# Steps of three batches moved in an attention and expert kernel, with another order of loads and turned copies at the end

## The reference

```python
def _L0_xattn_ref(query, key, value, adj, mask, ...):      # 16 heads of 16
    Q, K, V = heads(query, Wq, bq), heads(key, Wk, bk), heads(value, Wv, bv)
    scores = jnp.einsum('bhqd,bhkd->bhqk', Q, K) / jnp.sqrt(jnp.float32(D))
    scores = scores + adj[None, None, :, :]
    scores = jnp.where(mask == 0, jnp.float32(-jnp.inf), scores)
    weights = jax.nn.softmax(scores, axis=-1)
    out = jnp.einsum('bhqk,bhkd->bhqd', weights, V)
    out = out.transpose(0, 2, 1, 3).reshape(b, s, E)
    return jnp.einsum('bsf,ef->bsf', out, Wo.T) + bo

def _L0_ffn_ref(hidden_states, gate_w, w1, b1, w2, b2):    # 8 experts, 256 -> 1024 -> 256
    gate_probs = jax.nn.softmax(x @ gate_w.T, axis=-1)
    expert_idx = jnp.argmax(gate_probs, axis=-1)
    expert_w = jnp.take_along_axis(gate_probs, expert_idx[:, None], axis=1)[:, 0]
    for e in range(n_experts):
        ye = jax.nn.relu(x @ w1[e] + b1[e]) @ w2[e] + b2[e]
        sel = (expert_idx == e)[:, None]
        out = out + jnp.where(sel, ye * expert_w[:, None], 0.0)

x = x + jnp.tanh(g_xattn[0]) * _L0_xattn_ref(_layernorm(x), ctx, ctx, adj, mask, ...)
x = x + jnp.tanh(g_ffn[0]) * _L0_ffn_ref(_layernorm(x), gate_w, w1, b1, w2, b2)
```

## Time and profile before

| | |
|---|---|
| median of three runs | 571.88 us (569.12 to 575.5) |
| profiled execution | 572.78 us, a span of 570.8 us |
| mean granted clock of TensorE | 0.996 of full |
| TensorE matmul busy | 532.1 us, 93% of the span |
| TensorE weight load busy (beside matmul) | 405.8 us, 71% |
| VectorE, ScalarE, POOL busy | 298.7, 304.6, 304.2 us, 52 to 53% each |
| data moved | 77.22 MB, mean 135 GB/s |

### The profile page before, as it was taken

One profiled execution on the slowest core, in us unless ns is written; L12 is line 12 of the kernel. 1 busy time (PEld: TensorE's weight loads), 2 busy tenths in 40 slices (PEclk: granted clock), 3 DMA queues, 4 the chain that ended last, 5 costly groups with the idle time before them and its releaser, 6 DMA issues.

```text
span 570.8 us, 13582 instructions
## 1 busy us (share of the span) xinstructions
PE 532.1 (93%) x4126; PEld 405.8 (71%) x4127; DVE 298.7 (52%) x908; ACT 304.6 (53%) x675; POOL 304.2 (53%) x461
## 2 busy tenths in 40 slices
PE   7999999989999989999999998879997899999996
PEld 5576666657566657666666765548897899999995
DVE  2676677875577876576876878813510111111111
ACT  4466676666677566678665676443232233333331
POOL 6345476765466665467573646451425445544441
PEclk9999999999999999999999999989999999999999
DMA  8633526301216410105510078778137656555650
GB/s 280 206 107 101 170 87 201 103 20 48 101 39 201 131 41 1 76 18 167 177 49 1 28 247 213 161 258 313 57 37 279 195 166 163 189 196 192 198 186 6
DMA packets 51392, 77.22 MB, mean 135 GB/s; under 512 B 9945, under 2 KB 34601, under 8 KB 51209
## 3 DMA queue, kind: packets, MB, share of 16 engines
q1 hardware_dynamic: 46600, 67.72, 37.2%
q0 software_dynamic: 4096, 8.29, 5.2%
q10 hardware_dynamic: 640, 0.52, 0.3%
HBM read 52.76 MB, written 7.89 MB: 106 GB/s over the span
## 4 chain that ended last, share of the span: by engine, by line
PE 51%; DMA 18%; issue 10%; DVE 7%; POOL 5%; ACT 4%; SPq 4%; POOLq 1%; DVEq 0%; ACTq 0%
PE bank L941 13%; DMA out_y<-cT,sidx 10%; PE bank L953 9%; PE bank L931 7%; PE bank L834 4%; DVE prob L1551 3%; DMA slot_d<-pair,posi 3%; SPq L345 3%; PE bank L1116 2%; PE bank L869 2%; PE bank L915 2%; PE bank L1031 2%; PE bank L1106 2%; ACT pt L1209 2%; POOL rows L739 2%
## 5 line engine op out<-in xcount | busy, mean ns | idle before, releaser
L1551 DVE CUSTOM_DVE_ANT_0 prob<-bank,adjm 128x512 f32<-128x512 f32 x256 | 172.5, 687 | 82.1 <-issue 50.1
L672 POOL TENSOR_SCALAR prob<-prob,negmax 128x512 f32<-128x512 f32 x192 | 133.2, 698 | 130.6 <-DVE negmax L1551 125.7
L1209 ACT ACTIVATE pt<-bank 128x512 f32<-128x512 f32 x256 | 150.3, 594 | 87.6 <-PE bank L941 83.3
L941 PE MATMUL bank<-ident,prob 128*128 128x128 f32 x1024 | 154.8, 274 | 4.6 <-POOL prob L672 2.3
L941 PEld LDWEIGHTS bank<-ident,prob 128*128 128x128 f32 x1024 | 124.2, 141 | 43.5 <-issue 14.7
L1278 ACT ACTIVATE adjm<-bank,colsm 128x128 f32<-128x128 f32 x184 | 52.6, 368 | 107.5 <-PE bank L1106 86.0
L931 PE MATMUL bank<-w2s 128*128 128x512 bf16 x256 | 97.5, 381 | 7.6 <-DVE negmax L1551 4.9
L953 PE MATMUL bank<-pt,vals 128*32 128x256 f32 x1024 | 69.1, 389 | 0.7 <-DVE vals L1365 0.5
L1727 DVE TENSOR_TENSOR cT<-bank,maski 128x256 f32<-128x256 f32 x18 | 7.6, 424 | 117.3 <-PE bank L1116 103.3
L1106 PEld LDWEIGHTS bank<-xT,pt 128*128 128x128 f32 x576 | 67.1, 192 | 1.8 <-ACT xT L1272 1.0
L1106 PE MATMUL bank<-xT,pt 128*128 128x128 f32 x576 | 67.3, 275 | 0.7 <-ACT xT L1272 0.7
(11 more groups left out here) (192 smaller groups left out, 604.0 us busy)
## 6 DMA issues: line engine op xcount, KB each, us to landing
pt<-in_L_ffn_w SPq DMA_DIRECT2D x19, 1024.0 KB, 5.2
w2s<-parts SPq DMA_DIRECT2D x96, 128.0 KB
w2s<-in_L_ffn_w SPq DMA_DIRECT2D x8, 1024.0 KB, 9.9
maski<-in_mask_Bx1xSxS_ik SPq DMA_DIRECT2D x4, 1024.0 KB, 5.4
w2s<-parts SPq DMA_DIRECT2D x56, 64.0 KB, 2.1
xres<-in_x SPq DMA_DIRECT2D x18, 128.0 KB, 2.2
x_d<-rows SPq DMA_DIRECT2D x18, 128.0 KB, 1.7
xn_d<-rows SPq DMA_DIRECT2D x18, 128.0 KB, 2.5
```

What stands on the lines that cost most here:

```text
L672: po.tensor_scalar(prob[:, m], prob[:, m], -1.0, negmax[:, m:m + 1], ALU.mult, ALU.add).then_inc(s_shpool, 1)
L941: mm = pe.transpose(tr_bank[n % NTB][:, c * P:(c + 1) * P], prob[:, n % TILES % NB, c * P:(c + 1) * P], ident[:])
L1209: act.activation(pt[:, g % 2, :, j, q2 * P:(q2 + 1) * P], tr_bank[c % NTB][:].rearrange("p (c q) -> p c q", c=QT), ACT.Exp).then_inc(s_cac ...
L1551: ve.tensor_tensor_reduce(out=prob[:, m % NB], in0=sc_bank[m % NS][:], in1=adjm[:, qt], scale=-1.0, scalar=BIG, op0=ALU.add, op1=ALU.min, ...
```

## The change

In the first three batches, by the tables:

- the use "turn 1" goes from step 25 to 26, and "next k 0" from 26 to 27;
- "gate 0,1" goes from step 43 to 44, and "gate 3" from 66 to 68;
- the four slot scatters go from steps 53, 55, 57, 59 to 54, 59, 62, 67, and the wait for them from 72 to 73;
- the factor for the next but one batch's x goes from step 66 to 67, its normalization from 67, 69, 71, 73 to 69, 70, 72, 73.

In the last batch one slot scatter goes from step 45 to 46. At the end SP issues three w1 loads of the early groups ahead of the five slot reads (before: one ahead, two behind) and the w2 of experts 4 and 6 behind them (before: ahead of them). TensorE turns the rows of early group 1 ahead of the second half of the hidden layer of group 0, and ScalarE copies them in the same place. The first two w1 loads of the late groups go ahead of the first two late slot reads, and so ahead of the wait for the last scatters.

```diff
--- before.py
+++ after.py
@@ -94,14 +94,14 @@
     PRE = len(PRO)
     FIRST_NEXT = PRO.index("next x")
     NEXT = 8
-    TAIL_A = [(15, "heads", 0), (18, "heads", 1), (23, "turn", 0), (25, "turn", 1), (29, "out", 0),
-              (33, "out", 1), (38, "normed", 0), (41, "normed", 1), (43, "gate", (0, 1)), (51, "rank", 0)]
+    TAIL_A = [(15, "heads", 0), (18, "heads", 1), (23, "turn", 0), (26, "turn", 1), (29, "out", 0),
+              (33, "out", 1), (38, "normed", 0), (41, "normed", 1), (44, "gate", (0, 1)), (51, "rank", 0)]
     USES = sorted([(10, "values", 0), (11, "values", 1)] + TAIL_A
                   + [(12, "next x", 0), (14, "next x", 1), (17, "next ctx", 0), (19, "next ctx", 1),
-                     (21, "next q", 0), (26, "next k", 0), (30, "next q", 1), (35, "next k", 1)]
+                     (21, "next q", 0), (27, "next k", 0), (30, "next q", 1), (35, "next k", 1)]
                   + [(45, "heads", 2), (46, "heads", 3), (50, "turn", 2), (52, "turn", 3), (53, "out", 2),
                      (56, "out", 3), (61, "normed", 2), (63, "gate", (2,)), (64, "normed", 3),
-                     (66, "gate", (3,))], key=lambda use: use[0])
+                     (68, "gate", (3,))], key=lambda use: use[0])
     LAST_USES = sorted([(10, "values", 0), (11, "values", 1), (13, "heads", 0), (14, "heads", 1), (16, "turn", 0),
                         (18, "turn", 1), (20, "out", 0), (22, "out", 1), (27, "normed", 0), (29, "normed", 1),
                         (31, "gate", (0, 1)), (39, "rank", 0), (45, "heads", 2), (46, "heads", 3), (48, "turn", 2),
@@ -115,11 +115,11 @@
     OUT_RSTD = ({32: 0, 36: 1, 56: 2, 59: 3}, {23: 0, 25: 1, 55: 2, 57: 3})
     ROW_STEPS = ({36: 0, 39: 1, 59: 2, 63: 3}, {25: 0, 27: 1, 57: 2, 59: 3})
     SHIFT_STEP, EXP_STEP, PICK_STEPS = (45, 33), (46, 34), ((47, 48, 49), (35, 36, 37))
-    STATS_STEPS, RSTD_STEP, NORM_STEPS = (61, 62, 64, 65), 66, (67, 69, 71, 73)
+    STATS_STEPS, RSTD_STEP, NORM_STEPS = (61, 62, 64, 65), 67, (69, 70, 72, 73)
     CAST_STEPS = {n + VE_QK_AT + 1: (i, w, a) for i, (n, w, a) in enumerate(USES)
                   if w in ("next q", "next k")}
     SPLIT_STEPS = {n + 1: use for n, use in CAST_STEPS.items()}
-    SLOT_STEPS, SCATTERED_STEP = ((53, 55, 57, 59), (41, 43, 45, 47)), (72, 60)
+    SLOT_STEPS, SCATTERED_STEP = ((54, 59, 62, 67), (41, 43, 46, 47)), (73, 60)
     TABLE_STEPS = (41, 42, 43, 44, 45, 48, 49, 50, 51, 52, 57, 58)
     INDEX_STEP, NORMED_STEPS = TILES - 5, (TILES - 5, TILES - 2)
     ABS_STEPS = {29: 0, 34: 1, 40: 2, 45: 3}
@@ -479,18 +479,17 @@
                 sp.dma_start(ew1[u], w1_v[ds(e, 1)].rearrange("x p k f -> p (x k) f")).then_inc(e_w1[u], 16)
 
             sp.wait_ge(s_stack, last * STACKED)
-            sp.wait_ge(s_score, last * TILES + 6 * TILES // 8)
-            for e in range(X // 2, X, 2):
-                load_w2(e)
             sp.wait_ge(e_eid, 1)
-            early_w1(0)
+            sp.wait_ge(s_xT, B * 4)
+            for s in range(3):
+                early_w1(s)
             sp.wait_ge(r_scat, B * (16 * QT))
             for s in range(EARLY):
                 at = sp.value_load(base_i[0:1, s:s + 1], min_val=0, max_val=X * TOK)
                 sp.dma_start(slots[:, s], slot_d[ds(at, P), :]).then_inc(e_slots, 16)
-            sp.wait_ge(s_xT, B * 4)
-            for s in range(1, 3):
-                early_w1(s)
+            sp.wait_ge(s_score, last * TILES + 6 * TILES // 8)
+            for e in range(X // 2, X, 2):
+                load_w2(e)
             tail_pair(last, last * QT, 2, last * QT + 2)
             sp.wait_ge(s_score, B * TILES)
             for e in range(X // 2 + 1, X, 2):
@@ -520,11 +519,11 @@
                 sp.dma_start(w1s[:, v], w1_v[ds(e, 1)].rearrange("x p k f -> p (x k) f")).then_inc(f_w1[v], 16)
 
             sp.wait_ge(r_eid, 1)
+            for v in range(2):
+                load_w1(v, v)
             sp.wait_ge(r_scat, (B + 1) * (16 * QT))
             for v in range(2):
                 load_slots(v, v)
-            for v in range(2):
-                load_w1(v, v)
             with sp.Fori(0, LATE // 2 - 1) as i:
                 for v in range(2):
                     load_slots(i * 2 + (v + 2), v, i * 2 + v + 1)
@@ -1060,8 +1059,8 @@
             pe.wait_ge(s_osb, B * GROUPS + 2)
             last_tail("heads", 0)
             last_tail("heads", 1)
+            early_turn(1)
             early_hidden(0, 1)
-            early_turn(1)
             last_tail("turn", 0)
             last_tail("turn", 1)
             early_hidden(1, 0)
@@ -1294,8 +1293,8 @@
             act.wait_ge(e_eid, 1)
             e = expert_of(0)
             hidden(0, 0, e, 0)
+            turned_rows(1, 1)
             hidden(0, 0, e, 1)
-            turned_rows(1, 1)
             last_tail("turn", 0)
             last_tail("turn", 1)
             e = expert_of(1)
```

## The result

The change makes the kernel slower: 584.95 us (median of 4 runs, 583.37 to 588.54) against 571.66 us, a ratio of 1.024 with a 95% interval of 1.019 to 1.029. Run again with more rounds it gave 585.97 us and 1.025 (1.021 to 1.030). The forecast was 575 us with a range of 565 to 582: the time lies above it. The profiled execution has a span of 581.5 us, 10.7 more than before, and a clock of 0.991. Lines of the changed kernel are one lower than before from about 480 on.

The account below looks back on a forecast made before the run. TensorE was taken as the bound in the batches, chains of scatter, slot reads and gather at the end. +6.5 us in three batches and -3.7 at the end gave +2.8 on 572.78, or 575 us against the median, range 565 to 582.

Parts of the forecast that it names:

- The two moved uses: Three batches: new waits at "next q 1" and "next k 1", 1.75 then 3.83 us late in all; +11.5 us together.
- Gates, slot scatters, normalization: Three batches: waits at gates, behind slot scatters and for rstd go or shrink: -2.7, -1.5 and -0.8 us.
- The clock at the new waits: Slower rival: one clock fall of 1.8 us per batch at the new waits, none saved at the end; 581 us, chance 0.08.
- Late w1 loads ahead of the late slot reads ... I take 0: Late groups: loads leave the gather's time and enter the scatter's; taken as 0, between +1.9 and -2.8 us.
- The early end: Early groups: index -0.8, gather -1.0, clock -0.9, turned copy of slot 1 -1.0; together -3.7 us.
- The gather, taken 1.0 us shorter: After the early slot reads: 7.55 us before, now beside two other loads; -1.0 us, between 0 and -3.85.
- The estimate of when the loads would be in: Early end: 3.1 MB of w1 loads ahead of the slot reads all in at about 370.9 us.
- The gain of 0.8 us for the index: Early slot reads behind three w1 loads: index 0.8 us earlier, between -1.78 and +2.7.
- the fit that the prediction set beside this: Early w1 loads: 2.0 us plus bytes over 436 GB/s, in after 9.2 us at 368.5; sum 1.0 us lower.
- The sum: Whole kernel: +6.5 us in three batches, -3.7 at the end, +2.8 in all; 575 us against the median.
- The two slower rivals: Clock falls at the new waits, 581 us, chance 0.08; slot reads come late behind loads, 582 us, chance 0.10.
- reads behind loads (the late ones): Slower rival: slot reads late behind loads, +2.7 for -0.8, no gather or clock gain, +1.9 at late reads; chance 0.10.

Follow-up runs that it names:

- a_moves_back: The changed kernel with "turn 1" put back to step 25 and "next k 0" to 26, late order kept: 572.31 us, 1.000 to before.
- b_moves_only: The kernel before with only "turn 1" at step 26 and "next k 0" at 27: 582.36 us, 1.017 to before.
- change_again: The whole change run once more with more rounds, against the kernel before: 585.97 us, 1.025.
- a_both_back: The changed kernel with the two uses back at 25 and 26 and the late w1 loads back behind the late slot reads: 566.9 us, 0.992 to before.
- b_moves_steps: The kernel before with the two uses, gates, slot scatters and normalization moved, the whole end as before: 584.23 us, 1.017 to before.
- b_late_act: The kernel before with the first two late w1 loads issued by ScalarE on its own queue, ahead of early group 4's hidden layer: 577.1 us, 1.011 to before.

## Why the prediction was wrong, point by point

- **The two moved uses: right in mechanism, place and size.** 3.83 us per batch was the working; 3.67 to 3.71 was measured. Each link (tile, `rows`, `rest`; shift, factor, split) stood in the trace, and the two kernels that reorder VectorE and POOL took one wait away and cut the other.
- **Gates, slot scatters, normalization: near.** -5.0 was forecast; the batches of a_moves_back are 1.67, 1.52 and 1.37 us shorter than before, -4.6. The kernel with these steps alone gained 3.4 us.
- **The clock at the new waits: the wrong side of the choice.** I gave this rival 0.08 because the clock had held beside the 2.77 us ahead of the late loop. That was the exception: in eight of the other nine profiles with the old order of the late reads it fell at this place. After the wait of 2.0 us in the batches it fell in 8 of the 12 batches of the four profiles that have it together with the moved steps, and in none of the three of b_moves_only, which I can't explain. The price, 1.8 us, was right: 1.6 and 1.8 for the same batch with and without a fall. One execution in which the clock held says little about the next.
- **"Late w1 loads ahead of the late slot reads ... I take 0": the step that failed.** Its upper end, +1.9, was the slowing of the scatter alone. I let the early reads wait behind the loads and not the late ones, though they are the same order: loads issued while a scatter is under way, then reads. In the change the reads took 7.33 us, and TensorE's idle grew by 4.6 us to 7.39 (to 5.60 in the profile of change_again). The slowing that the bound was made of is not to be seen: the last scatter took 8.22 to 10.02 us in the six profiles with loads beside it and 8.05 to 9.93 in the ten without. By a_moves_back against a_both_back the late order costs 5.4 us, in the kernel before 3.0 (0.6 to 5.5).
- **The early end: -3.7 was too much.** The milestones of the one profile give -3.4, but the part alone gains 1.1 us (from 2.3 gained to 0.2 lost). The base was one execution: POOL's wait of 1.78 us in it is the longest of seven, and its fall of the clock at 382 us is missing in two of the other six with the same order. The gather, taken 1.0 us shorter, did not change. The estimate of when the loads would be in, 370.9 us, was good: the third landed at 379.1 and the reads at 380.0, in a kernel that is 7.8 us later there, so at 371.3 and 372.2. But the reads of before had landed at 371.9. The gain of 0.8 us for the index was not there; the estimate of the loads left out the reads behind them. The Trainium skill (DMA: Bandwidth & Descriptors, section on the anatomy of one DMA) states the fit that the prediction set beside this, 9.2 us for the three loads, for transfers issued by POOL; these are SP's, and took 11.9 us from the first issue.
- **The sum.** Forecast against the median +3.1, measured +13.3. Of the 10 us missing, the end has some 8 (+4.6 by the difference of change_again and b_moves_steps, where -3.7 stood), and the batches some 3 (+9.8 for +6.5), which falls of the clock would explain. The two shares come from different runs and are good to about 3 us. The two profiles in the table above, one of them the forecast's base, say much the same: 6.6 us more at the end than forecast, 1.6 more in the batches, where that profile has one fall. The two slower rivals came true in part and together, the fall of the clock and reads behind loads (the late ones); the prediction priced each by itself.

The Trainium skill (DMA: Bandwidth & Descriptors, section on queues, rings and completion order) says that each DMA engine takes turns between the queues that it has work for. By that rule the reads of b_late_act would have come in among the loads, if they had reached the engines by then, which no run shows. Here they took 5.87 us and came among the last quarter of the loads' packets only, and the measurement decides.

## What to carry to other kernels

When a use moves one step, follow its release on every engine that handles it: a step's order on VectorE or POOL can make one step of delay into two waits of 2 us. A small read that the next stage waits for does not belong behind large loads, here also not on another queue, and a load that was issued during a scatter hardly moved until the scatter had landed. A gain that is read from one execution's idle time holds only if other executions have that idle too.

## What the runs showed of the hardware

- While an indirect scatter of 4 x 128 small rows was under way, other transfers hardly moved: 26 and 66 GB/s with the DMA engines counted busy, against up to 391 GB/s once it had landed (in the kernel with ScalarE's loads 26, then 376). That the scatter is the cause was not tried alone.
- Reads of 1 KB took 5.87 us with 2 MB issued ahead of them on the other queue, and 7.33 us with 2 MB ahead on their own; with none ahead 1.72.
- A wait of 2.01 us in a row of matmuls was followed by a fall to the lower clock in 8 of 15 batches. Idle of 1.8 to 3.8 us ahead of the late loop was followed by one in 8 of 10 profiles, idle of 4.2 to 7.4 us in 6 of 6.
